# An 18-place weight ring on SyncE's queue, four sums that taper to two, and no holding operations, in a transformer block with 64 experts

## The chip, the cores and the metric

One core of a Trainium2 chip runs the whole program. Its engines are TensorE (PE), VectorE (DVE), ScalarE (ACT), GpSimd (POOL) and SyncE (SP); each works through its own instructions in order, and semaphores order them among each other. SP, ACT and POOL can start DMA transfers; each of the three has a queue of its own, and all three feed the same 16 DMA engines. The metric is the device time of one execution in microseconds (us). The three runs of this kernel lie within 0.2% of one another.

## The reference, cut to what matters

All numbers are float32. `x` is 4 batches of 512 tokens of 256 values. The block is modulated attention with 16 heads, then a modulated mixture of experts:

```python
h = layernorm(x) * (1 + ca) + sa
x = x + ga * attention(h)                       # 16 heads of 128, tanh-capped causal scores
h = layernorm(x) * (1 + cb) + sb
scores = softmax(h @ gate.T)                    # 2048 tokens x 64 experts
topk_w, topk_i = best 6 within the best 3 of 8 groups of experts
pos = running count of the tokens sent to the same expert
slot = expert * 96 + min(pos, 95)               # 96 rows for each expert; what is over shares the last row
buf[slot] = h[token]                            # 64 x 96 rows
out = (silu(buf @ Wg.T) * (buf @ Wu.T)) @ Wd.T  # one expert at a time, 176 wide
y = sum over k of out[slot] * topk_w
x = x + gb * (y + shared_expert(h))             # the shared expert is 352 wide
```

## The kernel before, in words

**Attention.** The four batches run one after the other, 16 heads each, in a hand-written software pipeline of one period for each head. In a period PE does the scores of head p, the projection of head p-1, and the query, key and value products of head p+2. ACT does the tanh and the exponential, POOL masks the probabilities (`mask`, two `affine_select`) and computes the reciprocal roots of the norms (`norms`, a `pow`), DVE does the rest. The second layer norm, the router and the slot numbers of batch b are done on DVE, ACT and POOL during the first 12 periods of batch b+1; those of the last batch run behind its last head, beside the shared expert on PE.

**Holding operations.** `hold` writes one column: on POOL a 128x1 product into `holdp`, on DVE a 128x1 memset into `holdv`. It stands behind a wait and ahead of the operation that needs it, in `norms`, `mask`, `ln_rstd`, the layer norms and the routing.

**Routing.** POOL scatters each token's row to `slot_rows` in HBM (`table`, L496, 96 indirect DMAs). Tokens over an expert's 95th go to its 96th row, which stands for the last such token: `lrow` holds these 64 rows. When all scatters have landed, SP writes `lrow` to `slot_rows` (L397), waits for it, and loads the 96 rows of the first 8 experts into the places `xg` (L400).

**Experts.** For expert e PE does: transposes of the rows of e+1 (`tr1`, L1490), the gate and up products of e (`gu`, L1497), transposes of the activations of e-1 (`tr2`, L1504), the down product of e-2 (`down`, L1512). ACT copies the transposed rows (L706), does the silu (L710) and writes the weighted result of expert e-2 to one of five places `orow` (L719). POOL then adds these 96 rows to a sum in HBM with an indirect DMA that accumulates (L554); every row of a sum is added to by its own DMA, and a DMA on a sum has to land before the next one on the same sum may start. There are three such sums (`acc`), taken in turn, up to expert 50 and two from 51 on (`ACUT`). A place `orow` is free when its scatter and the copy of its last row have landed.

```python
        def acc_of(e):
            return e % NACC if e < ACUT else e % 2
```

**Weights.** An expert's weights are `wgu` (gate and up) and `wd` (down). They lie in a ring of `RING` = 11 places. Five `wgu` places and four `wd` places have memory of their own and are filled in the first microseconds; the others lie in memory of the attention and are filled when batch 3's second residual is done (L389 to L392). Expert e+11's `wgu` is loaded by SP when `gu` of e is done (L404), its `wd` by ACT when `down` of e is done (L725). SP also copies the last row of each `orow` to HBM (`last_rows`, L408) and loads the third sum at e = 55 (L414); DVE scales it by `rgb` and adds it to `xs` in eight operations, six of them behind experts 58 to 63 (L1198, L1206).

**End.** When the last scatters of sums 0 and 1 have landed SP loads both (L430), DVE adds, scales and adds them to `xs` (L1219, L1221, L1224), with the rows over capacity from a product on PE (L1539, L1213), and SP writes `xs` out (L433).

Of the kernel before, what the change touches and what calls it, by code (L numbers as in the profile page):

```python
# [20 lines left out]
F32 = mybir.dt.float32  # L21
I32 = mybir.dt.int32
U32 = mybir.dt.uint32
F32R = mybir.dt.float32r
# [23 lines left out]
RING = 11  # L48
ACUT = 51
# [10 lines left out]
NACC = 3  # L60
# [6 lines left out]
def build(nc, x, wqkv, wo, qkw, cossin, ct, wmod, gate, sgu, sd, wgu, wd, out):  # L67
    with ExitStack() as ctx:  # L68
# [14 lines left out]
        o95_d = nc.dram_tensor("last_rows", (E, D), F32, kind="Internal").ap()  # L83
# [25 lines left out]
        hth = sb("hth", [P, KC, T], F32R)  # L109
        htl = sb("htl", [P, KC, T], F32R)  # L110
        wh = sb("wh", [P, KC, 3 * DH], F32R)
        wl = sb("wl", [P, KC, 3 * DH], F32R)
        xn = sb("xn", [P, TT, D])
        qth = sb("qth", [P, T], F32R)
        qtl = sb("qtl", [P, T], F32R)
        kth = sb("kth", [P, T], F32R)
        ktl = sb("ktl", [P, T], F32R)
        oth = sb("oth", [P, T], F32R)
        otl = sb("otl", [P, T], F32R)
# [65 lines left out]
        holdp = sb("holdp", [P, 5])  # L185
        warm = sb("warm", [P, 1])
        holdv = sb("holdv", [P, 8])
# [24 lines left out]
        def gu_place(v):  # L212
            return v.rearrange("p (k m) -> p k m", k=KC)

        def wd_place(v):
            return v.rearrange("p (m d) -> p m d", m=2)

        GW, DW, tail = 2 * KC * M, 2 * D, half + 4096
        wgus = [wge[:, u] for u in range(GEARLY)]
        wgus += [gu_place(prob[:, u * GW:(u + 1) * GW]) for u in range(2)]  # L220
        wgus += [gu_place(arena2[:, late + u * GW:late + (u + 1) * GW]) for u in range(2)]
        wgus += [gu_place(warena[:, tail + u * GW:tail + (u + 1) * GW]) for u in range(2)]
        wds = [wde[:, u] for u in range(EARLY)]
        wds += [wd_place(vx[0:MR, (u + 1) * DW:(u + 2) * DW]) for u in range(3)]
        wds += [wos[0:MR, c:c + 2, :] for c in (4, 6, 11, 13)]
        assert late + 2 * GW <= 4096 and len(wgus) == RING and len(wds) == RING
# [22 lines left out]
        iotat1 = sb("iotat1", [P, NT])  # L249

# [9 lines left out]
            wcol_rdy x_shared o95_ld o95_g cmb_ps cmb cmb2 outd""".split()  # L260
# [57 lines left out]
        def _(sp):  # L318
# [13 lines left out]
            for u in range(GEARLY):  # L332
                sp.dma_start(wgus[u], wgu[u]).then_inc(w_in[u], 16)
# [1247 lines left out]
```

## Time and profile before

| | us |
|---|---|
| median of 3 runs (1053.9 to 1055.69) | 1053.91 |
| the profiled execution: time | 1056.7 |
| the profiled execution: span of the trace | 1055.0 |
| TensorE busy in the span | 984.8 |
| attention, from the start to about | 770 |
| first transpose of the experts | 849.69 |
| last accumulating scatter starts | 1024.96 |
| loads of the last two sums start | 1029.08 |

The profiled execution took 1.7 us more than its span, and 2.8 us more than the median of the runs. Times of the trace are counted from the start of the span.

### The profile page before, as it was taken

The page shows a single profiled execution, that of the slowest core. Times are in us where ns is not written, and L with a number is a line of the kernel's source. Part 1 is how long each engine was busy: PE and PEld are TensorE (multiplying, and loading weights), DVE is VectorE, ACT ScalarE, POOL GpSimd, SP SyncE. Part 2 cuts the span into 40 slices and gives each one's busy share as a digit, 9 for nine tenths or more (in the row PEclk, how much of TensorE's full clock was granted, in tenths as well). Part 3 has the DMA queues.
Part 4 walks back from the last instruction along what each step waited for, and adds up shares of the span by engine and source line. Part 5 has one row for each costly group of instructions (what it writes and reads, how often), then busy time and mean ns, then how long its engine had stood idle before and what let it go on. Part 6 is the DMA issues. An engine that isn't in the chain of part 4 may idle for free. (4 is left out here: it accounts for less than half of the span.)

```text
span 1055.0 us, 18375 instructions
## 1 busy us (share of the span) xinstructions
PE 984.8 (93%) x6301; PEld 876.3 (83%) x6301; DVE 681.9 (65%) x1815; ACT 585.3 (55%) x1093; POOL 405.9 (38%) x599
## 2 busy tenths in 40 slices
PE   4999999999999999999999999999989799998973
PEld 4799999999999999999999999999865466555642
DVE  3566667778778876877887686887568132222356
ACT  2566766766676667676666767666531034333420
POOL 3122223223224554322455442235524424555560
PEclk9899999999999999999999999999999999999985
DMA  9992000001000101100010012000015169999957
GB/s 352 334 330 69 0 0 1 1 2 56 1 1 18 43 32 38 56 2 1 17 42 28 23 43 93 9 7 11 16 43 153 37 170 293 289 291 281 256 88 239
DMA packets 65289, 99.31 MB, mean 94 GB/s; under 512 B 8271, under 2 KB 46426, under 8 KB 64824
## 3 DMA queue, kind: packets, MB, share of 16 engines
q1 hardware_dynamic: 41192, 69.19, 21.3%
q0 software_dynamic: 11808, 12.87, 6.0%
q10 hardware_dynamic: 12208, 16.21, 4.9%
q8 instruction: 46, 0.75, 0.3%
q14 instruction: 35, 0.29, 0.1%
HBM read 66.11 MB, written 38.86 MB: 99 GB/s over the span
## 5 line engine op out<-in xcount | busy, mean ns | idle before, releaser
L442 POOL TENSOR_TENSOR holdp<-neghalf 128x1 f32<-128x1 f32 x145 | 31.5, 218 | 465.2 <-ACT prob L605 241.0
L599 ACT ACTIVATE prob<-ps,rn 128x512 f32<-128x512 f32 (+3 forms) x256 | 121.0, 526 | 124.2 <-PE ps L1317 116.5
L1291 PE MATMUL ps<-wh,hth 128*128 128x384 f32 x512 | 178.5, 349 | 5.2 <-DVE htl L791 3.1
L1291 PE MATMUL ps<-wh,htl 128*128 128x384 f32 x512 | 173.0, 338 | 0.0
L1291 PE MATMUL ps<-wl,hth 128*128 128x384 f32 x512 | 172.9, 338 | 0.0
L839 DVE TENSOR_REDUCE ss<-arena 128x8 f32<-128x1024 f32 x64 | 78.1, 1220 | 128.6 <-ACT arena L575 128.4
L1344 PE MATMUL ps<-vx,prob 128*128 128x129 f32 (+1 forms) x1280 | 153.5, 274 | 0.4 <-POOL prob L490 0.4
L1344 PEld LDWEIGHTS ps<-vx,prob 128*128 128x128 f32 x1280 | 148.6, 191 | 0.7 <-POOL prob L490 0.7
L575 ACT ACTIVATE arena<-ps 128x1024 f32<-128x1024 f32 x64 | 65.7, 1026 | 124.0 <-PE ps L1291 124.0
L554 POOL DMA_INDIRECT acc<-wos,arena x64 | 92.5, 1446 | 100.4 <-ACT wos L719 83.6
L496 POOL DMA_INDIRECT slot_rows<-pay,arena x96 | 97.6, 1017 | 42.9 <-issue 24.6
L480 POOL TENSOR_TENSOR rn<-rtmp,neghalf 128x8 f32<-128x8 f32 (+1 forms) x64 | 105.2, 1644 | 6.5 <-POOL rtmp L478 2.0
L1291 PEld LDWEIGHTS ps<-wh,hth 128*128 128x128 f32 x512 | 97.6, 191 | 6.7 <-DVE htl L791 3.5
L1291 PEld LDWEIGHTS ps<-wl,hth 128*128 128x128 f32 x512 | 97.7, 191 | 0.0
L1291 PEld LDWEIGHTS ps<-wh,htl 128*128 128x128 f32 x512 | 97.3, 190 | 0.0
L1317 PE MATMUL ps<-qth,kth 128*128 128x512 f32 (+3 forms) x256 | 87.7, 343 | 7.1 <-DVE arena L869 4.4
L1183 DVE TENSOR_TENSOR xn<-ps,arena 96x176 f32<-96x176 f32 x64 | 21.6, 337 | 106.6 <-ACT arena L710 79.5
L605 ACT ACTIVATE prob<-prob 128x1280 f32<-128x1280 f32 x64 | 83.6, 1306 | 0.0
L1317 PE MATMUL ps<-qth,ktl 128*128 128x512 f32 (+3 forms) x256 | 82.9, 324 | 0.0
L1317 PE MATMUL ps<-qtl,kth 128*128 128x512 f32 (+3 forms) x256 | 82.3, 321 | 0.0
L869 DVE TENSOR_TENSOR arena<-ps,arena 128x512 f32<-128x512 f32 x118 | 75.7, 682 | 3.4 <-PE ps L1332 3.4
L1332 PE MATMUL ps<-woh,oth 128*128 128x256 f32 x256 | 73.2, 286 | 1.5 <-DVE otl L855 1.5
(194 smaller groups left out, 2192.7 us busy)
## 6 DMA issues: line engine op xcount, KB each, us to landing
wge<-in_wgu SPq DMA_DIRECT2D x30, 352.0 KB
slot_rows<-pay SPq DMA_DIRECT2D x1, 6456.0 KB, 35.3
acc<-pay SPq DMA_DIRECT2D x3, 2048.0 KB, 19.0
arena<-slot_rows ACTq DMA_DIRECT2D x56, 100.9 KB
warena<-in_wqkv SPq DMA_DIRECT2D x1, 4992.0 KB, 20.3
prob<-in_wgu SPq DMA_DIRECT2D x12, 352.0 KB
arena<-in_wgu SPq DMA_DIRECT2D x12, 352.0 KB
warena<-acc SPq DMA_DIRECT2D x8, 512.0 KB, 8.6
```

The costliest lines, as they stand in the source:

```text
L480: pool.tensor_tensor(rn[:, bass.ds(head(n), 1), :].squeeze(1), rtmp[:], neghalf[:], ALU.pow).then_inc(s["r_rdy"], 1)
L496: pool.indirect_dma_start(buf_d, bass.IndirectOffsetOnAxis(ap=sloti[:, i * K + k:i * K + k + 1], axis=0), pay[:, i, :], None, bounds_check ...
L554: pool.indirect_dma_start(acc_d[acc_of(e)], bass.IndirectOffsetOnAxis(ap=tokc[:, e % TR:e % TR + 1], axis=0), orow[e % ORING], None, bound ...
L575: act_(sq, ps[:, 0:TT, 0:2 * DH].rearrange("p i (c d) -> p i c d", c=2), ACT.Square).then_inc(s["squared"], 1)
L599: act_(prob[:, OFF[j]:OFF[j] + w], sflat[:, OFF[j]:OFF[j] + w], ACT.Tanh, scale=rn[:, bass.ds(head(n), 1), TT + j:TT + j + 1].squeeze(1)). ...
L605: act_(prob[:, 0:1280], prob[:, 0:1280], ACT.Exp, scale=CAP).then_inc(s["expd"], 1)
L839: nc.vector.tensor_reduce(ss[:].rearrange("p (c i) -> p i c", c=2), sq, X, ALU.add).then_inc(s["ss_rdy"], 1)
L869: tt(ya, yp, ya, ALU.add).then_inc(s["y_added"], 1)
L1291: last = mm(ps[:, i, 0:3 * DH], hp[:, k, i * P:(i + 1) * P], wp[:, k, :], start=(k == 0 and m == 0), stop=(k == KC - 1 and m == 2))
L1317: last = mm(sflat[:, OFF[j]:OFF[j] + w], kp[:, j * P:(j + 1) * P], qp[:, T - w:T], start=(m == 0), stop=(m == 2))
L1332: last = mm(yps[:, i, :], op[:, i * P:(i + 1) * P], wp[:], start=(m == 0), stop=(m == 2))
L1344: last = mm(o, prob[:, c:c + P], vx[:, bass.ds((vslot(n) * TT + j) * (DH + 1), DH + 1)], start=(j == 0), stop=(j == i))
```

## The change

- The ring has 18 places. The float32r tiles of the attention (`hth`, `htl`, `wh`, `wl`, `qth`, ...) are allocated last and given free in the builder, and six `late_t` and four `late_*` tiles are laid over them; the rest of `arena2`, `rcur` and the old places serve too. SP fills places 5 and 6 of `wgu` after the start and the others step by step, as the memory of the attention becomes free.
- SP loads all `wd` of the ring, in its own queue (`down`), ACT none. ACT copies each `orow`'s last row straight to `o95` in SBUF; `last_rows` in HBM and its load at the end are gone.
- Four sums up to expert 37, three up to 49, two from 50 on. The fourth shares its memory in SBUF with sum 0: it is loaded at e = 42 of SP's loop, and DVE scales it and adds it behind experts 45 to 52. The third is loaded at e = 53 and added behind experts 56 to 63. One more sum is filled with zeros at the start.
- The 96th rows of the first 8 experts go straight from `lrow` to `xg`; their other 95 rows are loaded when the scatters have landed, without waiting for a write of `lrow`.
- No `hold`. POOL's loop over heads 2 to 11 of batch 0 is written out.

```diff
-RING = 11
-ACUT = 51
+RING = 18
+CUTS = ((38, 4), (50, 3), (64, 2))
-NACC = 3
+NACC = 4
...
+        accs.append(accs[0])
         def acc_of(e):
-            return e % NACC if e < ACUT else e % 2
+            return e % next(n for cut, n in CUTS if e < cut)
...
+            gate_ups(range(5, 7))
             sp.sem_inc(s["tab_free"], 1)
...
+            sp.wait_ge(s["qkv_rdy"], B * H)
+            gate_ups(range(7, 13))
+            sp.wait_ge(s["wol_rdy"], cnt(B - 1, H - 2))
+            downs(range(4, 8))
+            sp.wait_ge(s["s_rdy"], 3 * B * H)
+            downs(range(8, 12))
+            sp.wait_ge(s["o_rdy"], B * H)
+            gate_ups(range(13, 15))
+            downs(range(12, 15))
             sp.wait_ge(s["tabw"], 16 * TT * K * (B - 1))
             sp.sem_inc(s["tab_free"], 1)
+            sp.wait_ge(s["y_rdy"], 2 * B * H)
+            downs(range(15, 17))
+            sp.wait_ge(s["x2_rdy"], 2 * B + 1)
+            gate_ups(range(15, 17))
+            downs(range(17, 18))
...
+            for e in range(XR):
+                sp.dma_start(xg[C - 1:C, e, :], lrow[e:e + 1, :]).then_inc(xg_in[e], 16)
             sp.wait_ge(s["tabw"], 16 * NT * K)
-            sp.dma_start(buf_d...[:, C - 1, :], lrow[:]).then_inc(s["last_out"], 16)
-            sp.wait_ge(s["last_out"], 16)
             for e in range(XR):
-                sp.dma_start(xg[0:C, e, :], buf_d[e * C:(e + 1) * C, :]).then_inc(xg_in[e], 16)
+                sp.dma_start(xg[0:C - 1, e, :], buf_d[e * C:(e + 1) * C - 1, :]).then_inc(xg_in[e], 16)
...
-            def last_row(e):
-                sp.wait_ge(s["orow_rdy"], e + 1)
-                sp.dma_start(o95_d[e:e + 1], orow[e % ORING][C - 1:C, :]).then_inc(o95s[e % ORING], 16)
+            def down(e):
+                sp.wait_ge(s["dn_ps"], e + 1)
+                sp.dma_start(wds[e % RING], wd[e + RING]).then_inc(w_in[e % RING], 16)
+            def more_sum(a):
+                sp.wait_ge(ys[a], adds(a, E))
...
             for e in range(E + 2):
                 if e + RING < E:
                     gate_up(e)
                 if e >= 2:
-                    last_row(e - 2)
-                if e == ACUT + 4:
-                    third_sum()
+                    if e - 2 + RING < E:
+                        down(e - 2)
+                if e == 42:
+                    more_sum(3)
+                if e == 53:
+                    sp.wait_ge(s["cmb2"], B)
+                    more_sum(2)
...
-            def hold(c):
-                pool.tensor_tensor(holdp[:, c:c + 1], neghalf[:, 0:1], neghalf[:, 0:1], ALU.mult)
...
-            with pool.Fori(2, SIDE) as p:
+            for p in range(2, SIDE):
                 period(0, p)
...
-            def e_down(e):
-                a.wait_ge(s["dn_ps"], e + 1)
-                a.dma_start(wds[e % RING], wd[e + RING]).then_inc(w_in[e % RING], 16)
+            def e_last_row(e):
+                a.wait_ge(s["orow_rdy"], e + 1)
+                a.dma_start(o95[e:e + 1, :], orow[e % ORING][C - 1:C, :]).then_inc(o95s[e % ORING], 16)
...
+                for a, first in ((3, 45), (2, E - 2 * B)):
+                    if first <= e < first + 2 * B:
+                        n = e - first
+                        more_added(a, n // 2) if n % 2 else more_scaled(a, n // 2)
```

## Rows read from the trace of the kernel before

**Rows 1.** The page's first part: busy us, share of the span, instructions.

```profile
PE 984.8 (93%) x6301; PEld 876.3 (83%) x6301; DVE 681.9 (65%) x1815; ACT 585.3 (55%) x1093; POOL 405.9 (38%) x599
```

**Rows 2.** Stretches: length, busy time per engine, granted clock, DMA share, GB/s.

```profile
40.00:740.00 700.00, 690.01 (x4974) 678.31 (x4973) 529.28 (x1245) 476.40 (x825) 257.56 (x452) 1.00 0.13 41
740.00:849.70 109.70, 96.95 (x422) 65.98 (x420) 60.02 (x197) 29.95 (x55) 45.64 (x54) 0.95 0.21 57
880.00:980.00 100.00, 93.29 (x454) 57.81 (x453) 27.49 (x185) 38.91 (x114) 51.93 (x38) 1.00 1.10 290
980.00:1009.00 29.00, 29.00 (x147) 19.06 (x146) 13.44 (x64) 11.07 (x34) 15.10 (x11) 1.00 0.93 237
1029.00:1055.00 26.00, 8.46 (x20) 6.07 (x19) 17.92 (x15) 0.00 (x0) 0.00 (x0) 0.50 0.73 242
```

**Rows 3.** The chain that ended last, three of its DMA pieces: start, length.

```profile
939.13 6.12 DMA acc<-wos,arena
...
956.54 7.40 DMA acc<-wos,arena
...
1018.34 3.35 DMA acc<-wos,arena
```

**Rows 4.** Timeline of POOL: 7 of the 64 scatters, and one DVE operation.

```profile
857.43 1.51 POOL L554 DMA_INDIRECT acc<-wos,arena  x1 [23.32 <-ACT wos L719]
...
947.34 1.41 POOL L554 DMA_INDIRECT acc<-wos,arena  x1 [1.32 <-ACT wos L719]
...
956.54 1.41 POOL L554 DMA_INDIRECT acc<-wos,arena  x1 [2.14 <-ACT wos L719]
958.25 1.41 POOL L554 DMA_INDIRECT acc<-wos,arena  x1 [0.30 <-DVE arena L1176]
...
991.87 1.41 POOL L554 DMA_INDIRECT acc<-wos,arena  x1 [1.25 <-ACT wos L719]
994.10 1.41 POOL L554 DMA_INDIRECT acc<-wos,arena  x1 [0.83 <-DVE arena L1176]
...
1024.54 1.23 DVE L1206 TENSOR_TENSOR xs<-xs,warena 128x1024 f32<-128x1024 f32 x1
1024.96 2.08 POOL L554 DMA_INDIRECT acc<-wos,arena  x1 [0.30 <-issue]
```

**Rows 5.** Timeline of PE: the first transposes of two experts in a row.

```profile
858.26 0.33 PE L1490 MATMUL ps<-ident,arena 96*128 96x96 f32 x2
...
860.65 0.33 PE L1490 MATMUL ps<-ident,arena 96*128 96x96 f32 x2
```

**Rows 6.** Timelines ahead of the first expert, of POOL, SP, DVE and PE.

```profile
833.14 0.97 POOL L496 DMA_INDIRECT slot_rows<-pay,arena  x1 [0.30 <-issue]
...
837.32 3.61 SPq L400 DMA_DIRECT2D arena<-slot_rows  x8
...
837.56 1.29 DVE L1116 TENSOR_TENSOR warena<-ps,rgb 128x512 f32<-128x512 f32 x2 [10.22 <-remote]
...
849.69 0.39 PE L1490 MATMUL ps<-ident,arena 96*128 96x96 f32 x2 [0.78 <-DVE warena L1116]
```

**Rows 7.** Holding operations by line; and waits of PE, 40 to 740 us.

```profile
L442 POOL TENSOR_TENSOR holdp<-neghalf 128x1 f32<-128x1 f32 x145 | 31.5, 218 | 465.2 <-ACT prob L605 241.0
...
PE ps L1317 <- DVE arena L869: 4.4, 6, 1.2
...
PE ps L1344 <- POOL prob L490: 0.4, 1, 0.4
```

**Rows 8.** DMA issues by line: count, KB each, median us from issue to landing.

```profile
arena<-slot_rows ACTq DMA_DIRECT2D x56, 100.9 KB
...
warena<-acc SPq DMA_DIRECT2D x8, 512.0 KB, 8.6
wde<-in_wd ACTq DMA_DIRECT2D x20, 192.0 KB
...
wge<-in_wgu SPq DMA_DIRECT2D x30, 352.0 KB
```

More of the change, by code:

```diff
@@ L266, in build @@
         acc_in = [sem(f"acc_in{b}") for b in range(B)]
-        acc2_in = [sem(f"acc2_in{b}") for b in range(B)]
         block = ctx.enter_context(nc.Block())
@@ L331, in _, with gate_ups, downs @@
             sp.dma_start(gates[:], gate).then_inc(s["ld_gate"], 16)
-            for u in range(GEARLY):
-                sp.dma_start(wgus[u], wgu[u]).then_inc(w_in[u], 16)
-            for u in range(EARLY):
-                sp.dma_start(wds[u], wd[u]).then_inc(w_in[u], 16)
+            def gate_ups(us):
+                for u in us:
+                    sp.dma_start(wgus[u], wgu[u]).then_inc(w_in[u], 16)
+            def downs(us):
+                for u in us:
+                    sp.dma_start(wds[u], wd[u]).then_inc(w_in[u], 16)
+            gate_ups(range(GEARLY))
+            downs(range(EARLY))
             sp.wait_ge(s["fills"], 2)
@@ L419, in _ @@
                 if e >= 2:
-                    last_row(e - 2)
-                if e == ACUT + 4:
-                    third_sum()
+                    if e - 2 + RING < E:
[5 more added lines that the diff above has]
+                    more_sum(2)
+            sp.wait_ge(s["cmb2"], 2 * B)
+            for a in range(2):
+                sp.wait_ge(ys[a], adds(a, E))
             for u in range(ORING):
                 sp.wait_ge(o95s[u], 16 * len(range(u, E, ORING)))
-            sp.dma_start(o95, o95_d).then_inc(s["o95_ld"], 16)
-            for a in range(2):
-                sp.wait_ge(ys[a], adds(a, E))
             for b in range(B):
@@ L484, in mask @@
                 pool.wait_ge(s["expd"], cnt(b, n))
-                hold(0 if not isinstance(n, int) or n % 2 else 4)
                 d = prob[:].rearrange("p (a c) -> p a c", a=3)[:, :, 0:P]
@@ L737, in e_period @@
                 e_silu(e, base)
+                if e >= 3:
+                    e_last_row(e - 3)
                 if not (isinstance(base, int) and base + e < 2):
                     e_orow(e - 2, base) if e >= 2 or isinstance(base, int) else e_orow(e - 2 + XR, base - XR)
-                if e >= 2 and e - 2 + RING < E:
-                    e_down(e - 2)
                 if XR <= e + LEAD < E:
@@ L746, in _ @@
                 e_period(e, 0)
+            e_last_row(E - 3)
             e_orow(E - 2, 0)
+            e_last_row(E - 2)
             e_orow(E - 1, 0)
+            e_last_row(E - 1)
             for q in range(4):
```

129 lines of the change are left out of this document (58 added, 71 removed).

## The prediction

> **What bounds the kernel now.** I read the busy shares first [rows 1]: TensorE is busy for 93% of the span, which says only that few stages can be idle on it. The stretches say which [rows 2]. From 40 to 740 us, the attention, PE is busy 690.0 of 700 us at the full clock: nothing that another engine saves there can give back more than the 10 us that PE is idle. From 740 to the first expert at 849.7 it is busy 97 of 109.7. From 880 to 980, in the experts, PE is busy 93.3 of 100 us, and the DMA share is at its ceiling with 290 GB/s. From 1029 on PE and POOL are done, and DVE combines the sums. So the places to look at are the experts, the 110 us ahead of them and the 26 us behind them.
>
> In the experts PE's own pace is the distance of two first transposes in a row, 860.65 - 858.26 = 2.39 us for an expert [rows 5]. The first of the 64 scatters starts at 857.43. At PE's pace scatter 50 (counting from 0) would start at 857.43 + 50 x 2.39 = 976.9; it starts at 991.87 [rows 4]. So 15 us were lost by then, and what lost them is to be read in the chain that ended last [rows 3]: its long pieces are accumulating scatters, 6.12 and 7.40 us from the start of the instruction to the landing while weights stream, 3.35 us when they don't. In the timeline scatters 33 and 36, on the same sum, start at 947.34 and 956.54, 9.2 us apart, and scatter 30 starts at 939.13 by the chain, 8.2 us ahead of 33 [rows 3, 4]. Three sums in turn with one scatter each in 8.2 to 9.2 us make 2.7 to 3.1 us for an expert: more than PE's 2.39. The wait reaches PE by way of the five places for results, ACT's copy into them and the two PSUM banks behind that copy.
>
> The last part of this stretch is worse. From expert 51 on two sums are left. Scatter 51 starts at 994.10 and scatter 63 at 1024.96 [rows 4]: 30.9 us for 12 experts, 2.57 each, against 28.7 at PE's pace. The loads of the last sums start 4.1 us behind scatter 63, and 26 us later the span ends. So the end of the program hangs on scatter 63, and I work out when that one will start.
>
> **The change part by part.** *Holding operations.* POOL's 145 cost 31.5 us of POOL, 218 ns each [rows 7]. POOL is busy 257.6 of 700 us in the attention [rows 2] and PE waited for its masks 0.4 us in all [rows 7]; what PE waits for there is DVE, 4.4 us at the one line shown. So the cover is PE itself. What can come back is a part of the layer norm's and the routing's chains at the turn of each batch, where DVE and POOL shed a few short operations: at most the 0.4 + 4.4 us of the two rows, at least nothing. I take 1 us. The loop that POOL no longer runs as a loop costs nothing for the same reason, and the fourth fill of zeros at the start (2 MB on SP's queue, 7 us of transfer at 290 GB/s) lies beside an attention that needs no DMA: DMA share 0.13 [rows 2]. It is waited for at head 12 of batch 0. Nothing.
>
> *Filling the ring.* SP now issues 13 `wgu` and 14 `wd` loads in the tail of the attention and behind it: 13 x 352 + 14 x 192 KB = 7.4 MB, 26 us at 290 GB/s [rows 2, 8]. Behind the waiting SP stand only `tab_free`, the copy of `h2` and the rows of the experts. The stretch from 740 to 849.7 moved only 57 GB/s, so there is room, and the loads that wait for the last heads are issued ahead of the second norm, not behind it. The first expert is not released by them. It is released by the shared expert: PE's transposes at 849.69 waited 0.78 us for L1116, while POOL's last scatter of rows was issued at 833.14 and SP loaded the rows from 837.32 on [rows 6]. Dropping the write of `lrow` and the wait for it takes about 2 us out of SP's chain (837.32 against a last scatter ending at 834.1), but 849.69 - 837.32 = 12.4 us of cover lie over it. So the start of the experts stays: 0, with a gain of nothing to the whole of that cover kept for a rival.
>
> *ACT and SP.* ACT drops the `wd` issues and takes the copies of last rows; SP the reverse. Both wait for work that is just done; ACT is busy 38.9 of 100 us and SP only issues. Nothing. The load of `last_rows` at the end goes; DVE had time for it ahead of the last scatter.
>
> *Four sums up to expert 37.* With four in turn, 8.2 to 9.2 us make 2.05 to 2.3 us for an expert, under 2.39: PE sets the pace. Scatter 37 then starts at 857.43 + 37 x 2.39 = 945.9 instead of 958.25 [rows 4]: 12.4 us earlier.
>
> *Three up to 49.* 8.2 / 3 = 2.73 for 12 experts is 4.1 us behind PE's pace.
>
> *The fourth sum's load.* This is the new wait, and it is the one I trust least. SP queues it behind expert 42's weights, DVE needs its first quarter behind expert 45, and DVE runs in order: if the quarter isn't there, all of the experts' DVE work stands. The first expert's gate product ends one pace behind its transposes, 849.69 + 2.39 = 852, and there the first reload is asked for; expert 45's ends at 852.1 + 45 x 2.39 = 959.6 [rows 5, 6]. Ahead of the quarter the queues have to move 43 `wgu` (15.5 MB), 41 `wd` (8.1), some 45 sets of rows (4.6) and 44 scatters of up to 96 KB (4.1), and the quarter itself (0.5): 32.8 MB. At 290 GB/s from 852 that is 113 us, 965; with the 237 GB/s of the later stretch it would be 990, but that stretch had less to move. Four sums let PE ask for 0.75 MB in each 2.39 us, 314 GB/s, more than the 290 that were seen with the share at its ceiling, so the backlog is real. A wait of 965 - 960 = 5 us, of which PE's work ahead in the PSUM banks hides one or two. The bounds are 0 and, with the 30 us of 237 GB/s, 30. The wait lets the scatters catch up, so it and the 4.1 us of three sums don't add: I take 5 us for both. Scatter 50 then starts at 857.43 + 119.5 + 5 = 981.9 and 51 at 984.3, instead of 994.10: 9.8 us ahead. The weights themselves aren't late: 18 places are 43 us of PE's work.
>
> *Two sums from 50.* Before, 51 to 63 took 30.9 us, with the load of the third sum in it; that load is in it again, and DVE's eight operations on the third sum now all fall into it, instead of six. A scatter that starts inside such an operation takes 2.08 us on POOL instead of 1.41 [rows 4], 0.7 more, and a chain passes two more of them at most: 1 us. Scatter 63 starts at 984.3 + 30.9 + 1 = 1016.2, instead of 1024.96: 8.7 us earlier. PE alone, held up 5 us once, would allow 857.43 + 63 x 2.39 + 5 = 1013, so it is the two sums that set it, and not PE.
>
> The Trainium skill, "SBUF — State Buffer", section "Who interferes with whom", says that a DVE operation with two SBUF inputs and a GpSimd instruction that reads SBUF exclude each other for the whole instruction. The two rows at the end of [rows 4] agree: the scatter that starts 0.42 us into a DVE addition took 2.08 us. By that rule the fourth sum's additions behind 45 to 52 would cost up to 0.7 us a scatter too, which a chain of three has room for only in part; scatter 63 would start at 1017.
>
> *The end* is DVE's and is as long as before: 26 us.
>
> Sum against the profiled execution: 1056.7 - 1 - 8.7 = 1047.0. The runs' median lies 2.8 us under it: 1044.
>
> **The rivals.** *A: the DMA queues set the pace, not the count of sums.* For it: the share is at the ceiling through the experts. Then the gain is the traffic that goes: seven experts' weights, 3.8 MB, less the fourth sum, 2.1 MB, 1.7 MB at 290 GB/s = 6 us. Time 1048. Against it: PE kept its 29.0 of 29 us from 980 to 1009 [rows 2] while weights still streamed.
>
> The Trainium skill, "DMA: Bandwidth & Descriptors", section "Queues, rings and completion order", has each DMA engine take turns between the queues. Here `wd` goes from ACT's queue to SP's, so a scatter would share with one stream of weights and not two. No row of before shows it; if its landing fell towards 5.5 us, three sums would do at PE's pace and the time would be 1041. I leave it 0.1 of the forecast's chance.
>
> *B: two sums for one expert more.* If the loads of weights are pushed later and fill the stretch from 984 to 996, the chains of two see 8 us for each scatter for two turns more than before, where the unloaded turn is 3.35 + 0.9: 2 x 2 us to 2 x 3 us. Time 1049 to 1051. For it: the backlog above.
>
> *C, on the other side: the fourth sum's quarter comes late.* DVE stands behind expert 45 until it lands. The forecast is used up when the wait is 10 us longer than I take, at a landing of 975, which means 32.8 MB at 267 GB/s or less. At 250 GB/s it lands at 983, scatter 50 starts near 998 and the time is some 6 us over before: 1060. For it: ACT's row loads and the last-row copies make many small packets. Against it: 290 GB/s are the mean of 100 us.
>
> *D: the stall ahead of the experts goes.* DVE waited 10.22 us until 837.56 for something the profile calls remote [rows 6], with PE in the shared expert. If the new placement or the missing holding operations undo it, the experts start when their rows are there, near 841, 9 us earlier: 1035. Nothing in the rows ties it to what is changed.
>
> **How the numbers follow.** The forecast, 1041 to 1047, gets 0.48; A 0.17; B 0.12; C 0.11; D 0.06; 0.04 for an effect so small that less than 0.2% (2.1 us, about what a measurement of this kernel can tell from no change) is left, and 0.02 for unseen harm. Faster is the forecast with A, B and D, 0.83; the same 0.04; slower 0.13. The range has to take in A and B on the one side and D on the other: 1035 to 1051.
>
> **What would show it.** Scatter 37 at 946 and gates 2.39 us apart up to expert 37: four sums right. First transposes at about 849: the start right. A wait of DVE for the load of the fourth sum of 3 to 6 us at about 960: the backlog right; near 0 would put the time at 1041, over 12 would make it slower. Scatter 63 at 1016 and a tail of 26 us behind its landing. A granted clock of 0.5 in PE's stretch during the wait would add to C.

## The result and the profile after

The change makes the kernel faster, by less than was forecast. Twenty runs of each have a median of 1050.72 us after (1045.62 to 1056.61) and 1053.76 before (1051.43 to 1057.45); the ratio is 0.9968, interval [0.9953, 0.9982]. That is 3.0 us, inside 1.9 to 5.0, where 9.9 were forecast. The profiled execution of after took 1047.1 us with a span of 1045.4, so it is 3.6 us under its median, while that of before was 2.9 us over its own.

The first part of the page, and then the stretches with the columns of [rows 2]:

```profile
PE 981.5 (94%) x6301; PEld 876.0 (84%) x6301; DVE 689.3 (66%) x1783; ACT 586.2 (56%) x1093; POOL 382.4 (37%) x454
```

```profile
40.00:740.00 700.00, 691.25 (x4992) 680.16 (x4991) 529.67 (x1218) 478.47 (x831) 235.93 (x316) 1.00 0.14 45
740.00:849.70 109.70, 95.35 (x398) 61.74 (x397) 58.25 (x186) 27.12 (x51) 43.07 (x47) 0.94 0.28 85
880.00:980.00 100.00, 95.20 (x471) 62.77 (x470) 36.84 (x203) 40.95 (x118) 55.06 (x39) 0.98 1.09 298
980.00:1009.00 29.00, 28.55 (x142) 18.69 (x141) 19.35 (x67) 11.90 (x34) 18.69 (x12) 1.00 0.61 132
```

The timeline of POOL answers to [rows 4]: scatters 0, 37, 50, 51 and 63.

```profile
856.06 1.51 POOL L581 DMA_INDIRECT acc<-wos,arena  x1 [25.47 <-ACT wos L746]
...
944.31 1.41 POOL L581 DMA_INDIRECT acc<-wos,arena  x1 [0.98 <-ACT wos L746]
...
986.07 1.41 POOL L581 DMA_INDIRECT acc<-wos,arena  x1 [2.94 <-ACT wos L746]
990.09 1.41 POOL L581 DMA_INDIRECT acc<-wos,arena  x1 [2.62 <-DMA acc<-wos,arena]
...
1016.04 1.41 POOL L581 DMA_INDIRECT acc<-wos,arena  x1 [0.63 <-issue]
```

Read alone, this looks like the forecast come true: scatter 37 at 944.3 (945.9 forecast), 63 at 1016.04 (1016.2). Only 50 came at 986.1 instead of 981.9. The new wait is in DVE's timeline, and SP's shows what the load of the fourth sum cost SP:

```profile
963.95 1.23 DVE L1218 TENSOR_TENSOR warena<-warena,rgb 128x1024 f32<-128x1024 f32 x1 [6.56 <-DMA warena<-acc]
```

```profile
950.17 0.33 SPq L439 DMA_DIRECT2D wos<-in_wd  x1
950.54 9.80 SPq L445 DMA_DIRECT2D warena<-acc  x4
960.39 2.20 SPq L435 DMA_DIRECT2D late_h<-in_wgu  x1
```

SP needed 9.8 us to issue the four DMAs while weights streamed; for the third sum in r17, at 971.43, it needed 2.33 us. That the queue was still full of weights is my reading and isn't shown by itself. The first quarter landed 13.4 us behind its issue. The chain that ended last goes through this load (first fence), and PE's timeline shows what it cost PE (second fence):

```profile
950.54 13.38 DMA warena<-acc
...
965.84 0.52 PE ps L1524 x2
966.36 1.71 PE ps L1532 x4
...
970.21 0.87 PE ps L1532 x4
```

```profile
958.66 1.03 PE L1532 MATMUL ps<-late_t,xn 88*96 88x256 f32 x4
...
965.84 0.52 PE L1524 MATMUL ps<-ident,xn 96*88 96x96 f32 x2 [4.80 <-DVE xn L1207]
966.15 1.92 PE L1532 MATMUL ps<-late_t,xn 88*96 88x256 f32 x4
...
970.04 1.03 PE L1532 MATMUL ps<-late_t,xn 88*96 88x256 f32 x4
...
972.43 1.03 PE L1532 MATMUL ps<-late_t,xn 88*96 88x256 f32 x4
```

DVE stood for the quarter, and PE stood 4.80 us for DVE. Behind the wait PE's granted clock was 0.60 from 966 to 970, after 1.00 until 964: the same four products took 1.71 us of the chain instead of 0.87. From the down product at 958.66 to the third one behind it PE took 13.8 us instead of 3 x 2.39, so it lost 6.6 us. No accumulating scatter stands in this chain between 929.72 and 1016.04.

The timeline of PE ahead of the experts answers to [rows 6]:

```profile
822.76 1.45 PE L1401 MATMUL ps<-warena 128*128 128x512 f32 x3
825.41 0.59 PE L1401 MATMUL ps<-warena 128*128 128x512 f32 x1 [1.20 <-issue]
827.51 0.59 PE L1401 MATMUL ps<-warena 128*128 128x512 f32 x1 [1.51 <-issue]
...
842.09 5.46 PE L1470 MATMUL ps<-wos,warena 128*128 128x256 f32 x24 [1.41 <-DVE warena L910]
848.33 0.39 PE L1510 MATMUL ps<-ident,arena 96*128 96x96 f32 x2 [0.79 <-DVE warena L1136]
```

The shared expert's products, 0.43 us apart elsewhere, come 1.4 to 2.8 us apart from 825 to 834, and in before they have such gaps from 831 on. In after the granted clock also fell, to 0.50 from 830 to 835. This hides from the experts part of what was won ahead of them, as the experiments show.

### The profile page after: what moved, and what is told of

Same layout as the page of the kernel before. It is cut to its first block, busy times and chain, and to the rows that moved or that the text cites. A ratio compares the mean times of both kernels' runs of the same rounds, so it can differ in the third digit from the quotient of the medians.

```text
span 1045.4 us, 18164 instructions
## 1 busy us (share of the span) xinstructions
PE 981.5 (94%) x6301; PEld 876.0 (84%) x6301; DVE 689.3 (66%) x1783; ACT 586.2 (56%) x1093; POOL 382.4 (37%) x454
## 4 chain that ended last, share of the span: by engine, by line
PE 78%; DVE 12%; issue 3%; DMA 3%; ACT 3%; POOL 1%; SPq 0%; POOLq 0%; DVEq 0%
PE ps L1311 22%; PE ps L1364 12%; PE ps L1337 11%; PE ps L1352 7%; PE ps L1517 7%; PE ps L1532 5%; PE ps L1401 3%; PE ps L1320 2%; PE ps L1323 2%; PE ps L1344 2%; DMA warena<-acc 1%; PE ps L1470 1%; ACT prob L626 1%; PE ps L1510 1%; PE ps L1524 1%
## 5 line engine op out<-in xcount | busy, mean ns | idle before, releaser
L515 POOL TENSOR_SCALAR_AFFINE_SELECT prob<-prob 128x384 f32<-128x384 f32 x64 | 35.4, 554 | 256.4 <-ACT prob L632 256.4
L524 POOL DMA_INDIRECT slot_rows<-pay,arena x96 | 99.4, 1035 | 43.2 <-issue 24.7
L509 POOL TENSOR_TENSOR rn<-rtmp,neghalf 128x8 f32<-128x8 f32 x64 | 105.3, 1645 | 5.3
L507 POOL TENSOR_SCALAR rtmp<-ss 128x8 f32<-128x8 f32 x64 | 12.5, 195 | 216.8 <-DVE ss L863 216.5
## 6 DMA issues: line engine op xcount, KB each, us to landing
slot_rows<-pay SPq DMA_DIRECT2D x1, 6456.0 KB, 34.4
```

What stands on the lines that cost most here:

```text
L509: pool.tensor_tensor(rn[:, bass.ds(head(n), 1), :].squeeze(1), rtmp[:], neghalf[:], ALU.pow).then_inc(s["r_rdy"], 1)
L524: pool.indirect_dma_start(buf_d, bass.IndirectOffsetOnAxis(ap=sloti[:, i * K + k:i * K + k + 1], axis=0), pay[:, i, :], None, bounds_check ...
```

## The experiments

Eighteen kernels ran, in five groups (r1 to r4, r5 to r8, r9 to r12, r13 to r16, r17 and r18), each group on a chip of its own beside runs of before. In the first two groups before had medians of 1052.8 and 1053.4 us, in the other three of 1045.1 to 1045.5. I compare within a group by ratios to before. Each kernel has one profile, and profiles are compared by the lengths of three stretches in us: from the start of scatter 0 to that of 37, on to 50, and on to 63. The column "first transposes" has the start of the experts:

| kernel | ratio, interval | first transposes | 0 to 37 | 37 to 50 | 50 to 63 | sum |
|---|---|---|---|---|---|---|
| before | | 849.69 | 100.8 | 33.6 | 33.1 | 167.5 |
| r5 before | 0.9998 [0.9979, 1.0016] | 851.49 | 97.0 | 34.0 | 32.7 | 163.7 |
| r11 before | 1.0007 [0.9991, 1.0023] | 841.08 | 97.0 | 34.4 | 32.7 | 164.1 |
| after | 0.9968 [0.9953, 0.9982] | 848.33 | 88.2 | 41.8 | 30.0 | 160.0 |
| r1 after | 0.9941 [0.9917, 0.9965] | 848.32 | 88.2 | 39.4 | 34.3 | 161.9 |
| r12 after | 0.9955 [0.9937, 0.9972] | 836.26 | 88.2 | 40.2 | 34.1 | 162.6 |
| r16 after | 0.9938 [0.9919, 0.9957] | 838.13 | 88.2 | 40.0 | 35.4 | 163.6 |
| r2 no holds | 0.9983 [0.9961, 1.0006] | 845.95 | 98.3 | 35.2 | 32.3 | 165.8 |
| r3 sums as before | 0.9978 [0.9959, 0.9997] | 848.96 | 99.6 | 29.7 | 33.8 | 163.1 |
| r4 fourth added later | 0.9943 [0.9921, 0.9965] | 848.20 | 88.2 | 41.5 | 35.6 | 165.3 |
| r6 no scatters of batch 3 | 0.9862 [0.9828, 0.9895] | 837.61 | 88.2 | 38.5 | 34.0 | 160.7 |
| r7 ring of 11 | 1.0040 [1.0018, 1.0061] | 848.72 | 88.2 | 44.1 | 35.7 | 168.0 |
| r8 three sums to 52 | 0.9978 [0.9958, 0.9998] | 848.84 | 88.2 | 43.9 | 37.9 | 170.0 |
| r9 four sums to the end | 0.9813 [0.9793, 0.9833] | 837.88 | 88.2 | 31.0 | 29.5 | 148.8 |
| r10 pause in the scatters | 1.0011 [0.9990, 1.0031] | 841.08 | 88.2 | 44.3 | 34.6 | 167.1 |
| r13 fourth sum not loaded | 0.9913 [0.9881, 0.9944] | 839.32 | 88.7 | 34.7 | 34.3 | 157.7 |
| r14 fourth on ACT's queue | 1.0023 [0.9993, 1.0053] | 838.92 | 88.2 | 43.5 | 35.0 | 166.8 |
| r15 both sums on it | 1.0011 [0.9981, 1.0041] | 839.08 | 88.2 | 43.2 | 33.8 | 165.2 |
| r17 fourth loaded, not added | 0.9940 [0.9917, 0.9962] | 838.20 | 88.2 | 41.4 | 32.6 | 162.2 |
| r18 fourth sum in four steps | 0.9954 [0.9937, 0.9970] | 838.98 | 88.2 | 44.3 | 29.5 | 162.0 |

**The change again, and its parts.** r1 is after unchanged.

> The changed kernel once more, to see what differs between its executions: 20 runs lay between 1045.6 and 1056.6 us, and the profiled one, 1047.1, shows every step where it was forecast. Theory 1 (the steps are right, the spread hides them: each execution has one or two waits of changing length): a second profile with a time near 1051 shows the same expert pace of 2.39 us but a longer wait for the fourth sum behind expert 45 (over 10 us instead of 6.6), or a later first expert (over 852). Theory 2 (a lasting harm that the first profile happened not to have): the pace itself is slower, 2.45 us or more. Median 1051 for both.

The ratio is 0.9941, and two later groups give 0.9955 and 0.9938: the change is worth 3 to 6.5 us. The first measurement is the low end of that. Neither theory fits: the pace up to 37 is the first profile's, and so are DVE's wait (6.7 us) and the start. But here PE lost more behind this wait: it stood 4.9 us, its granted clock was 0.58 from 966 to 974, and it lost 8.4 us in all, where the first profile lost 6.6.

r2 is before without `hold`, its calls and its two tiles, and with POOL's loop written out as in after:

```diff
-            def hold(c):
-                pool.tensor_tensor(holdp[:, c:c + 1], neghalf[:, 0:1], neghalf[:, 0:1], ALU.mult)
```

> The kernel before without any holding operation, and with POOL's loop over heads 2 to 11 written out; nothing else. The forecast's step says a gain of 0 to 2 us, ratio 0.998 to 1.000. The rival: the holding operations kept something in step, and without them the attention or the stage ahead of the experts loses; that would be a ratio of 1.003 or more and would eat a part of the forecast's 10 us.

Its interval touches 1, so the time says little. The marks along the trace say more: PE's gate product of batch 3 (the router's) starts at 786.63, and in before and after at:

```profile
788.54 1.90 PE L1361 MATMUL ps<-gates,arena 128*128 128x64 f32 x16
```

```profile
785.03 1.90 PE L1381 MATMUL ps<-gates,arena 128*128 128x64 f32 x16
```

By these three profiles the holding operations and the loop are worth 1.9 us of the 3.5 that the attention became shorter. The mark lies between 788.5 and 790.2 in the three profiles of before and between 783.8 and 785.7 in the four of after, so the split is uncertain by more than a microsecond.

r3 is after with the sums as before, the third one loaded at e = 55:

```diff
-CUTS = ((38, 4), (50, 3), (64, 2))
+CUTS = ((51, 3), (64, 2))
-NACC = 4
+NACC = 3
```

> The changed kernel with the sums of before: three up to expert 50, two from 51 on, no fourth sum and no load of it. If the gain comes from four sums, this one loses it: experts at 2.5 us and more, scatter 63 near 1024, a median at or over 1053. If DMA traffic sets the pace (rival A), it is faster than the changed kernel by the 2.1 MB of the fourth sum, 7 us: 1044. If the wait for the fourth sum takes in a usual execution what the four sums give, it is within 2 us of the changed kernel.

The four sums are worth 0.9978 against 0.9941, some 4 us with intervals that overlap, and no more. r4 adds the fourth sum behind experts 48 to 55:

```diff
-                for a, first in ((3, 45), (2, E - 2 * B)):
+                for a, first in ((3, 48), (2, E - 2 * B)):
```

> The changed kernel with DVE's eight operations on the fourth sum behind experts 48 to 55 instead of 45 to 52; its load is asked for at the same place. Theory 1: DVE gets 7.2 us more before it needs the first quarter, so the wait of 6.6 us there vanishes in most executions, the experts keep 2.39 us past 47; the third sum's load is asked for later, at 54, and its first quarter may be late by 2 to 4 us at 56, where PE has slack. Median 1046 to 1048, and a smaller spread. Theory 2: no change within 1 us.

DVE's wait fell from 6.6 us to 3.8 and 1.1 us, PE's wait for it from 4.8 to 2.0 us, scatter 50 came at 985.7 (986.1 and 983.7 in after and r1), and the ratio is r1's. In its chain a scatter of 9.56 us, from 970.21 on, stands behind DVE's wait (the profile is of the slowest of its nine runs). So the wait holds PE up in after, but making it shorter brings scatter 50 no earlier: the scatters take its place.

**The spread of before, the scatters of rows, the ring, a later cut.** r5 is before unchanged.

> The kernel before once more, for a second profile of it, since its first profiled execution (1056.7 us) was 2.9 us over the median of its 20 runs. Theory 1 (the forecast measured its gain from a late execution of before): this profile is near 1053, with the experts' first transpose at 846 to 848 instead of 849.69, or scatter 63 nearer than 167.5 us behind scatter 0; so a part of the 8.7 us was never there to be gained. Rival: it shows the same stages as the first one, and the offset is somewhere else in the span.

From scatter 0 to 37 it took 97.0 us, and 97.0 again in r11; the execution that I forecast from took 100.8. It was a long one by 3.8 us in just the stretch that I counted on. r6 leaves out batch 3's scatters of rows, and SP's wait for them:

```diff
-            for i in range(TT // 2):
-                pool.wait_ge(s["slot_rdy"], TT * (B - 1) + i + 1)
-                table(ik[i * K:(i + 1) * K])
...
-            for i in range(TT // 2, TT):
-                pool.wait_ge(s["slot_rdy"], TT * (B - 1) + i + 1)
-                table(ik[i * K:(i + 1) * K])
```

> The changed kernel without POOL's 24 scatters of batch 3's rows to the slots (left out: those rows never reach their experts, so the output differs where they should have; all later work runs on the same shapes). Between about 815 and 833 us PE gets one product of the shared expert in 2.1 us instead of 0.43, and it recovers 3 us behind the last of these scatters, in each of six profiles. If the scatters cause it, PE has no such stretch here, the first expert's transposes come at 838 to 841 instead of 848.3, and the median falls by 7 to 10 us, to 1040. If it is something of PE's own (its instructions, its clock), the stretch stays and the time is within 2 us of 1048.6.

The ratio is 0.9862 (the output lacks batch 3's rows in their experts). The slow stretch of PE is gone; the first transposes come 10.7 us earlier than in after, and 11.1 earlier than in r7 on the same chip:

```profile
822.93 7.03 PE L1395 MATMUL ps<-warena 128*128 128x512 f32 x16
831.37 5.46 PE L1464 MATMUL ps<-wos,warena 128*128 128x256 f32 x24 [1.40 <-DVE warena L904]
837.61 0.39 PE L1504 MATMUL ps<-ident,arena 96*128 96x96 f32 x2 [0.78 <-DVE warena L1130]
```

r7 is after with 11 places (`RING = 11`, the others unused).

> The changed kernel with 11 places instead of 18, all else kept: four sums, all weights in SyncE's queue, no holding operations, early filling. If the ring matters, PE waits for weights or the backlog puts the fourth sum later: seven more loads in the stretch, 3.8 MB at 290 GB/s, 13 us of queue; the first quarter of the fourth sum lands past 975, and the time is over 1053. If the number of sums alone sets the pace and 11 places are enough, the time is that of the changed kernel within 2 us, 1047 to 1050.

It is slower than before. With fewer places the weights are asked for later, so they still stream at 282 GB/s from 985 to 1000 where after moves 159. DVE waits 7.5 us for the fourth sum and 7.7 us for the third too, and PE stands 5.7 and 5.9 us for DVE. PE waited for no weights, here or in after. So the ring earns nothing by feeding PE; it earns by getting the weights out of the way of the sums.

r8 keeps three sums up to 52.

```diff
-CUTS = ((38, 4), (50, 3), (64, 2))
+CUTS = ((38, 4), (53, 3), (64, 2))
```

> The changed kernel with three sums up to expert 52 instead of 49 and two from 53 on; the third sum's load is asked for at 56 instead of 53 and its last two additions come behind the experts. In the changed kernel's profiles 13 scatters from 37 to 50 took 39 to 42 us and the 12 from 51 to 63 took 26 to 29. If the chain of scatters sets the end, three experts at a third of a loaded scatter (3.0 us) instead of a half (4.3) give 3 to 4 us: 1045. If PE or the load of the third sum sets it, nothing, or 1 to 2 us slower, since the load then falls nearer to the end.

Its one profile, of the slowest of its 12 runs, has DVE waiting 11.9 us for the fourth sum. Nothing is gained: 0.9978.

**What four sums would give, the pause, and both kernels again.** r9 keeps four sums to the end (`CUTS = ((64, 4),)`), without `more_sum` and its operations, so two sums are missing from its output:

> The kernel after with four sums in turn for all 64 experts; the third and the fourth sum are left out of the output (their loads and their 16 DVE operations are gone), so it shows what pace is left when a scatter never waits for its sum. Theory 1 (the chain of scatters on a sum sets the pace behind expert 37, and nothing else): scatters follow PE's 2.39 us to the end, the first at 856.0, number 37 at 944.3, 50 at 975.4, 63 at 1006.5, which is 10 to 11.5 us ahead of the 1016.0 and 1018.0 seen; time near 1037. Theory 2 (the DMA engines set the pace in the second half, my rival A): scatter 63 not before 1012, with PE waiting for weights; time 1043 or more. Theory 3 (the end of the program is set by something other than scatter 63): the span shrinks by less than scatter 63 moves.

The stretch from 860 to 980:

```profile
860.00:980.00 120.00, 120.00 (x605) 79.55 (x604) 37.50 (x252) 52.79 (x151) 71.03 (x51) 1.00 1.02 268
```

PE is busy for all of the 120 us while the weights and rows stream. So this traffic alone does not set the pace, and rival A is out: what after loses from 37 on, 13 us against r9, is lost to the number of sums, to their loads and to what waits for them.

r10 lets POOL wait between two halves of batch 3's scatters:

```diff
             for i in range(TT // 2, TT):
+            pool.wait_ge(s["sdn_ps"], 5)
```

> The kernel after, with one wait more: GpSimd stands between the 12th and the 13th of the last 24 scatters of batch 3 until PE has done the first half of the shared expert's down product of batch 2 (about 820.3 in the profile after), so that no more than 13 indirect DMAs follow one another, and the last is issued at about 834.5 instead of 829.7. Theory 1 (PE slows when some 18 of them have been issued back to back, so a backlog is the cause): no slow stretch of PE behind 822; the first transposes of the experts come at 840 to 843 instead of 848.3, time 5 to 8 us under that of after. Theory 2 (PE slows in these products whenever GpSimd scatters): the stretch lasts until some 3 us behind the last scatter, 838, and the first transposes come at 852 to 853: 4 to 5 us over. Theory 3 (it isn't the number but the last scatter's landing that is waited for): first transposes near 853 too, with PE at its pace of 0.43 us until then.

It couldn't answer. On this group's chip after has no slow stretch to begin with; r12's PE:

```profile
821.59 7.03 PE L1401 MATMUL ps<-warena 128*128 128x512 f32 x16
...
836.26 0.39 PE L1510 MATMUL ps<-ident,arena 96*128 96x96 f32 x2 [0.78 <-DVE warena L1136]
```

The pause only made the rows late: PE stood 3.8 and 0.7 us ahead of its first two transposes (the profile names the rows for the 0.7 alone), and the time is 5 us over r12's. r11 and r12 are before and after unchanged.

> The kernel before once more, for one profile more of it: does its experts' stage take 167.5 us from the first to the last scatter, as in the execution that I predicted from, or 163.7 us, as in the second one? Theory 1 (the first profile was a long one): 162 to 166 us. Theory 2 (the second was a short one): 166 to 169 us. The ratio to the kernel before is 1.000 within its interval.

> The kernel after once more, for a third profile: first to last scatter took 160.0 and 161.9 us in two of them. Theory 1 (a usual execution loses more in the stretch of three and two sums than the first profile): 162 to 165 us, time 1049 to 1052. Theory 2 (the first profile is usual and the gain is lost elsewhere): 160 to 162 us, with the first scatter or the tail later than 856.1 and 29.4 us.

**What is given back between 37 and 50.** r13 leaves out the fourth sum's load and DVE's operations on it:

```diff
-                if e == 42:
-                    more_sum(3)
...
-                for a, first in ((3, 45), (2, E - 2 * B)):
+                for a, first in ((2, E - 2 * B),):
```

> The kernel after with the same sequence of four, three and two sums, but the fourth sum is left out of the output: neither its 2 MB load at expert 42 nor its eight DVE operations behind experts 45 to 52 are there. Theory 1 (the load and DVE's wait for it cost what is lost in this stretch): scatter 37 to scatter 50 takes 33 to 35.5 us instead of 39.4 to 41.8, and the time is 5 to 7 us under that of after. Theory 2 (three sums in turn with scatters of 7 to 9 us do it alone): 38 to 40 us, as with the load; time 0 to 2 us under after.

34.7 us, 3.6 behind PE's pace: three sums alone cost that, and the fourth sum's load or its operations cost 5 to 7 us more. In time r13 is 3.7 us under r16 (medians 1034.89 and 1038.54, four runs each; the intervals of their ratios overlap), less than the 5 to 7 expected. So this price rests mainly on the profiles, one of r13 against four of after and one of r17. r17 has the load again and leaves only DVE's operations out.

> As r13, but the fourth sum is loaded at expert 42 on SyncE's queue as in after; only DVE's eight operations on it are left out. Theory 1 (the 2 MB in the stretch where weights and rows still stream are the cost): 38 to 42 us from scatter 37 to scatter 50, time as after or up to 2 us under it. Theory 2 (DVE's operations are the cost: its wait and the longer scatters beside them): 34 to 36 us as in r13, time 1034 to 1036 on a chip where before takes 1045.

41.4 us: the load costs this much even where no operation of DVE waits for it. The stretches of r13, and then of r17, show how:

```profile
949.00:967.00 18.00, 17.43 (x87) 11.30 (x86) 5.20 (x35) 7.67 (x23) 9.11 (x7) 1.00 0.95 225
967.00:985.00 18.00, 18.00 (x93) 11.90 (x92) 10.06 (x41) 7.39 (x22) 10.85 (x7) 1.00 0.79 188
```

```profile
949.00:967.00 18.00, 16.55 (x84) 10.74 (x83) 5.09 (x35) 6.00 (x18) 8.44 (x6) 1.00 1.11 297
967.00:985.00 18.00, 14.69 (x74) 9.30 (x73) 7.65 (x33) 5.83 (x18) 7.03 (x5) 1.00 0.88 227
```

Without the load the queues begin to empty from 949 on (225 GB/s, share 0.95), with it the share stays at its ceiling of 1.11 until 967. The chain of r17 has four scatters one behind the other there, the last one beside the third sum's load, which SP issued at 971.43:

```profile
941.31 9.21 DMA acc<-wos,arena
...
951.37 8.23 DMA acc<-wos,arena
...
960.45 8.87 DMA acc<-wos,arena
...
971.88 8.12 DMA acc<-wos,arena
```

8.1 to 9.2 us, where before had 6.12 and 7.40 [rows 3]. Not all of that is the load's: one scatter in the chain of r13 took 8.65 us too. The starts of the first three lie 10.1 and 9.1 us apart, 3.4 and 3.0 us for an expert with three sums, instead of the 2.73 that I took. From there the wait goes back to PE: from 935 to 985 ACT waits 12.1 us for scatters that hold the places `orow`, and PE 4.8 us for ACT.

This is r17's way and not after's. In all four profiles of after the chain goes through the quarter's load and DVE's wait, as in the section above, and ACT's waits for scatters from 930 to 1010 add up to 1.4 to 2.7 us (20.5 in r17):

| | DVE waits | PE waits for DVE | PE lost in all | 37 to 50, behind PE's 31.1 |
|---|---|---|---|---|
| after | 6.56 | 4.80 | 6.6 | 10.7 |
| r1 | 6.71 | 4.94 | 8.4 | 8.3 |
| r12 | 7.50 | 5.73 | 9.2 | 9.1 |
| r16 | 8.07 | 6.31 | 8.7 | 8.9 |

"PE lost in all" is the time from the last down product ahead of the wait to the third behind it, less 3 x 2.39. It is more than PE's wait because the granted clock behind the wait was 0.5 to 0.6 for 4 to 8 us. In three of the four profiles it is all that the stretch lost, within 0.2 us; in the first one scatter 50 comes another 4 us late, off the chain. In r17, where PE stood at most 2.4 us at a time for ACT, the clock stayed at 1.00 from 944 to 986.

r14 has ScalarE issue this load, behind expert 40, and r15 the third sum's too, at 53:

```diff
+            def more_sum(n):
+                a.wait_ge(ys[n], adds(n, E))
+                for b in range(B):
+                    a.dma_start(accs[n][:, b * TT:(b + 1) * TT], ...).then_inc(acc_in[b], 16)
```

> The kernel after, but ScalarE issues the four loads of the fourth sum, behind expert 40, instead of SyncE behind expert 42's weights; they no longer stand behind the weights in SyncE's queue, where the first quarter took 14 to 18 us. Theory 1 (the wait for the quarter is what costs): the quarter is there before DVE asks, the wait of 6.6 to 7.5 us is gone, scatter 50 comes 3 to 5 us earlier, time 3 to 4 us under after. Theory 2 (the 2 MB are the cost, wherever they are queued, because scatters and expert rows share the DMA engines with them): the wait goes but scatters get longer, 37 to 50 still takes 39 us or more, time within 1 us of after. Theory 3: rows of experts queue behind the sum on ScalarE's queue and PE waits for them: slower than after.

> As r14, with the third sum's four loads at expert 53 on ScalarE's queue too. No weights are left to be loaded by then, so by either theory this second move is worth little: within 1 us of r14; if the rows of the last experts are held up behind it, 1 to 3 us slower than r14.

DVE no longer waits, but the stretch is longer than in after, 43.5 and 43.2 us, and both kernels are slower than r16 (1.0023 and 1.0011 against 0.9938). The timeline of ACT in r14:

```profile
937.67 2.86 ACTq L762 DMA_DIRECT2D warena<-acc  x4
940.58 0.33 ACT L731 ACTIVATE arena<-ps 128x192 f32<-128x192 f32 x1 [4.12 <-issue]
940.64 7.03 ACTq L750 DMA_DIRECT2D vx<-wos  x1
940.81 0.30 ACT L735 ACTIVATE arena<-ps 96x176 f32<-96x176 f32 x1
947.85 0.47 ACT L744 ACTIVATE wos<-ps,arena 96x256 f32<-96x256 f32 x1 [6.74 <-issue]
```

The copy of one row, 1 KB, behind the four loads took 7.03 us to issue, and ACT, which is on the path, stood for it. So r14 does not test DVE's wait alone: it puts a stand of ACT in its place. On SP the 9.8 us of issuing held no engine up for weights, as the ring of 18 covered them. r16 is after unchanged.

> The kernel after as the control on the same chip: 0.994 to 0.997 of before; 39 to 42 us from scatter 37 to scatter 50.

r18 has SyncE issue the quarters one at a time, at experts 40, 42, 44 and 46.

```diff
-                if e == 42:
-                    more_sum(3)
+                if e in (40, 42, 44, 46):
+                    more_sum(3, ((e - 40) // 2,))
```

> The kernel after, but SyncE issues the four quarters of the fourth sum one at a time, at experts 40, 42, 44 and 46, instead of all four at 42. Theory 1 (the wait of 6.6 to 8.1 us and the burst are the cost, and spreading the burst helps): DVE's wait falls under 3 us, scatter 37 to 50 takes 36 to 38 us, time 2 to 4 us under after. Theory 2 (the bytes are the cost wherever they go): 39 us or more and a time within 1 us of after.

DVE waits 1.8, 4.1 and 1.8 us instead of about 7 once, the chain has scatters of 8.88, 8.63 and 9.38 us, 37 to 50 takes 44.3 us, and the ratio is after's. Spreading the load out gained nothing. None of the kernels that compute everything is faster than after by more than the intervals.

## Why the prediction was wrong in size

*Direction and mechanism* were right: faster, by way of the four sums, with SP's queue late for the fourth. Two terms of the sum were mis-sized: what four sums gain up to 37, taken from one long execution of before, and what is lost from 37 to 50.

*"1056.7 - 1 - 8.7", taken from one execution.* The stage from scatter 0 to 63 took 167.5, 163.7 and 164.1 us in three profiles of before, a mean of 165.1, and 160.0, 161.9, 162.6 and 163.6 in four of after, a mean of 162.0. The term of 8.7 us measured 3.1. The first profile of before was 3.8 us long from 0 to 37, and the first of after the shortest of four. That pair comes within 1.3 us of the 8.7 and hides the error; by luck both profiles lay to that side. For the same reason the last step, taking 2.8 us off because the median lay under the profile, was an assumption: after's profile lay 3.6 us under its median.

*Four sums up to 37* was right: 88.2 us in each of the four profiles of after, and 88.4 forecast. PE's 2.39 us is the pace. What this gains is 10.0 us by the mean of before's profiles, 98.3, and 8.8 by the two shorter ones, not 12.4.

*"I take 5 us for both"* is the step that failed. I had 4.1 us for three sums, and 5 us for DVE's wait with one or two of them hidden from PE, and let the one hide the other: 36.0 us from 37 to 50. It took 39.4 to 41.8, a mean of 40.3, which is 9.3 us behind PE's 31.1. Before takes 34.0 there, so the change gives back 6.3 us of its 10. Letting one hide the other was right; both sizes were too small. *The wait:* DVE stood 6.6 to 8.1 us instead of 5, of which 1.8 were hidden, as I took. (Of the bytes ahead of the quarter, 44 scatters of 96 KB are 4.3 MB and not 4.1, under 1 us of landing.) PE stood 4.8 to 6.3 us. Behind that the granted clock was low for some microseconds, which cost PE 1.8 to 3.5 us more. I had named a clock of 0.5 as a sign, but put it at nothing in the sum. *The scatters:* three sums alone cost 3.6 us (r13), near my 4.1, but beside the load 10.3 (r17, which has no wait of DVE), and that I had not priced. So the load costs about the same either way. In after the wait stands in the chain; where it is made shorter or taken out (r4, r17, r18) the scatters do. This is also why none of these kernels gained. The mean of 9.3 is near the sum of the 4.1 and the 5 only by chance.

*Two sums from 50*: 30.0 to 35.4 us, a mean of 33.4, against 34.3 forecast and 32.8 before; with the 10.0 and the 6.3 this makes the 3.1. The term for scatters beside DVE's operations can't be seen in a time. The Trainium skill, "SBUF — State Buffer", section "Who interferes with whom", is borne out by rows (in after, scatters 48 and 49, which start within DVE's scaling and addition of the fourth sum, took 2.40 and 2.08 us instead of 1.41), but r17, without eight of DVE's operations, has a stage of 162.2 us against 162.6 and 163.6.

*Rounds between queues.* The Trainium skill, "DMA: Bandwidth & Descriptors", section "Queues, rings and completion order", has each DMA engine take turns between the queues. From that I drew that scatters might land faster with one stream of weights less. The rows say otherwise: in r3, which has all weights in SP's queue and loads no fourth sum, the chain's scatters before 970 took 6.8 to 8.9 us, against 5.3 to 7.4 in before. The ring is deeper at the same time, so the rule itself isn't disproved; its use here was.

*Start of the experts and holding operations.* I gave 1 us and "no change". The attention became 3.5 us shorter (788.54 to 785.03; 4.2 by the means of three and four profiles), more than I took. Without a slow stretch the experts start 3.0 to 4.8 us earlier (r11 against r12 and r16). With it PE needs 25.6 us from the product at 822.76 to the first transposes instead of r12's 14.7, and before needed 23.4 from 826.31 on (r11 14.7), so 2.2 of the 3.5 are lost and 1.4 arrive. Filling the ring cost nothing, and the tail, from scatter 63 on, is 29.4 us instead of 29.5 to 30.1.

Together, start, stage and tail give 5 us where the slow stretch is (1.4 + 3.1 + 0.4), and up to 8.3 where it isn't; the four ratios give 3.4 to 6.5. Profiles of seven executions can't settle the difference. What makes an execution of after long or short between 37 and 50 is in part how long the clock stays low behind DVE's wait (6.6 to 9.2 us lost); for the stretch from 50 to 63, and for before's 97.0 or 100.8, it stays open.

*Rivals.* A fell with r9. B did not come: from 50 to 63 after took 0.6 us more than before, where B had 4 to 6. Slow scatters like B's stand in the chain one stretch earlier, and there only where DVE's wait is shorter or gone. C, a quarter past 975, did not come either: it landed at 963.93, against 965 forecast. But the low clock that I had counted with C came with the shorter wait too. D, the stall going, happened on other chips and to both kernels alike, so it is no effect of the change.

## What to carry to other kernels

A chain's profile is one execution: where a gain is the difference of two stretches limited by DMA latency, take a second profile of the kernel before and use the shorter one as the floor. When a large load comes beside streaming weights, price both ways in which it can hold up the busiest engine: the wait of the engine that needs the load, with the slower clock behind that wait, and the small DMAs that it makes slower. The longer one sets the time, and making one of them shorter uncovers the other. A large load belongs on the queue of an engine that has nothing else to do.

## What the runs showed of the hardware

- PE's matmuls of 128x512 came 1.4 to 2.8 us apart instead of 0.43 beside the last of POOL's 24 indirect DMAs, which it issued 1.28 us apart; in after, from 820 to 830, the DMA share was 0.02 to 0.03, and DVE and ACT were idle. The granted clock then fell, to 0.50 and 0.55 from 830 to 840. Without those DMAs (r6) all this was gone, worth 10.7 us at the first transposes. In the runs of the later groups it was absent with them, in both kernels. What in the scatters does it, and why only in the first two groups, wasn't found.
- PE's granted clock was 1.00 until it stood 4.80 to 6.31 us in the four profiles of after, and 0.5 to 0.6 for 4 to 8 us behind that. In r17, where it stood 2.4 us for ACT at most, it stayed at 1.00.
- Issuing four loads of 512 KB took SP 9.8 us while weights streamed, and 2.33 us later in r17; the 1 KB copy behind such loads took 7.03 us on ACT.
- From its start to its landing an accumulating scatter of 96 rows took 5.3 to 7.4 us in the chain of before while weights stream, 6.8 to 8.9 us in r3 and r13 (18 places, no load of the fourth sum), 8.1 to 9.2 us beside loads of sums in r17, and 3.35 us with nothing beside it [rows 3].
